# A closing projection that starts tile by tile in other PSUM banks, the last pair's transposes moved between the halves of its second unit, and finer waits in the first unit

## What is computed

```python
x = x + gnn(layernorm(x))     # 16 heads of 64; q, k, v projected twice; mask from 6144 edges
x = x + ffn(layernorm(x))     # 8 heads of 128, 8 experts per head, top 2 of them by a router
# in gnn, after the softmax:
out = attn @ v2               # 384 x 1024, two heads (a "pair") are 128 features
out = out @ wo.T + bo         # the closing projection
```

## Time and profile before

| | |
|---|---|
| median of 3 runs | 820.71 us (820.56 to 820.72) |
| the profiled execution | 820.65 us, of it the span from first to last instruction 818.9 us |
| TensorE busy | 808.5 us, 99% of the span |
| TensorE weight loads | 641.6 us, 78% |
| VectorE, ScalarE, GpSimd busy | 486.6, 370.3, 459.1 us |
| mean granted TensorE clock | 0.998 of full speed |
| moved by DMA | 153.50 MB, mean 187 GB/s |

### The profile page before, as it was taken

The page is one execution under the profiler, slowest core; times in us unless marked ns, Lnnn a source line. Parts: engine busy times, 40 slices in busy tenths (PEclk is TensorE's granted clock), DMA queues, the critical chain, the costliest instruction groups (busy, mean ns, idle before and its releaser), DMA issues.

```text
span 818.9 us, 13740 instructions
## 1 busy us (share of the span) xinstructions
PE 808.5 (99%) x4944; PEld 641.6 (78%) x4944; DVE 486.6 (59%) x1110; ACT 370.3 (45%) x599; POOL 459.1 (56%) x297
## 2 busy tenths in 40 slices
PE   8999999999998999999999999999999999999998
PEld 8999998988886779898588588588588488488476
DVE  7898860446564256998545545645645645645545
ACT  5433332566665343244634634535535535535531
POOL 4787776342423425557664664674664664664652
PEclk9999999999999999999999999999999999999999
DMA  8776565621222329634697696697697697697684
GB/s 295 201 218 186 187 167 159 204 90 66 78 79 71 104 79 341 204 107 144 134 265 264 142 284 237 145 264 257 145 270 250 136 269 257 141 256 261 150 219 171
DMA packets 73481, 153.50 MB, mean 187 GB/s; under 512 B 9520, under 2 KB 30640, under 8 KB 73424
## 3 DMA queue, kind: packets, MB, share of 16 engines
q1 hardware_dynamic: 59200, 120.93, 42.8%
q0 software_dynamic: 10944, 24.82, 16.8%
q10 hardware_dynamic: 3280, 6.98, 3.3%
HBM read 122.06 MB, written 37.97 MB: 195 GB/s over the span
## 4 chain that ended last, share of the span: by engine, by line
PE 96%; DVE 1%; DMA 1%; issue 1%; ACT 0%; POOL 0%; SPq 0%; DVEq 0%
PE bank L1651 26%; PE bank L1653 25%; PE bank L1652 25%; PE bank L1990 12%; PE bank L1706 2%; PE bank L1794 2%; PE bank L1769 2%; PE bank L1699 1%; DMA x<-in_x 1%; DVE stats L985 0%; PE bank L1741 0%; POOL rstd L538 0%; DVE x L1190 0%; PE bank L1747 0%; PE bank L1744 0%
## 5 line engine op out<-in xcount | busy, mean ns | idle before, releaser
L606 POOL TENSOR_TENSOR w_lo<-w_raw,w_hi 128x1024 fp32r<-128x1024 f32 x67 | 165.7, 2476 | 137.2 <-ACT w_hi L866 130.3
L1651 PE MATMUL bank<-w_hi,hT_hi 128*128 128x512 f32 x480 | 190.4, 397 | 4.1 <-DVE neg_mx L1127 3.2
L1653 PE MATMUL bank<-w_hi,hT_lo 128*128 128x512 f32 x480 | 188.2, 392 | 0.0
L1652 PE MATMUL bank<-w_lo,hT_hi 128*128 128x512 f32 x480 | 187.9, 391 | 0.0
L546 POOL TENSOR_TENSOR w_lo<-w_raw,w_hi 128x1024 fp32r<-128x1024 f32 x39 | 93.2, 2398 | 102.8 <-ACT w_hi L698 96.0
L866 ACT ACTIVATE w_hi<-w_raw 128x1024 fp32r<-128x1024 f32 x84 | 88.7, 1056 | 127.5 <-PE bank L1653 91.7
L1651 PEld LDWEIGHTS bank<-w_hi,hT_hi 128*128 128x128 f32 x480 | 91.0, 189 | 24.1 <-DVE neg_mx L1127 3.5
L1651 PE MATMUL bank<-hT_hi,w_hi 128*128 128x384 f32 x320 | 107.9, 337 | 0.0
L1652 PE MATMUL bank<-hT_lo,w_hi 128*128 128x384 f32 x320 | 107.0, 334 | 0.0
L1653 PE MATMUL bank<-hT_hi,w_lo 128*128 128x384 f32 x320 | 107.0, 334 | 0.0
L1653 PEld LDWEIGHTS bank<-w_hi,hT_lo 128*128 128x128 f32 x480 | 90.5, 188 | 19.3
(11 more groups left out here) (236 smaller groups left out, 1295.0 us busy)
## 6 DMA issues: line engine op xcount, KB each, us to landing
w_raw<-in_units SPq DMA_DIRECT2D x137, 512.0 KB
late<-in_units SPq DMA_DIRECT2D x56, 512.0 KB
w_raw<-in_units SPq DMA_DIRECT2D x16, 256.0 KB
scratch<-slots_scratch SPq DMA_DIRECT2D x7, 512.0 KB, 7.0
scratch<-in_src_row ACTq DMA_DIRECT2D x8, 384.0 KB
scratch<-in_dst_row ACTq DMA_DIRECT2D x8, 384.0 KB
sums_scratch<-zeros SPq DMA_DIRECT2D x1, 1536.0 KB, 8.0
sums_scratch<-x SPq DMA_DIRECT2D x1, 1536.0 KB, 10.6
```

The source lines that it names most:

```text
L606: pool.tensor_tensor(w_lo[:, s, :], w_raw[:, s, :], w_hi[:, s, :].bitcast(fp32), ALU.subtract).then_inc(lo_ready[s], 1)
L1651: pe.matmul(dst, a_hi, b_hi, start=first, stop=False)
L1652: pe.matmul(dst, a_hi, b_lo, start=False, stop=False)
L1653: return pe.matmul(dst, a_lo, b_hi, start=False, stop=last)
```

## The change

The first half of the closing projection is accumulated in banks 7, 6, 0 and the second in banks 3, 4, 5. Its unit 0 goes tile by tile (all six passes of a token tile together), starts after `oT_lo_done` of pair 6, and waits before the third tile alone for the first head's `max_ready`. Unit 1 is cut in two halves of 9 passes: head 0 of pair 7 is transposed between them, head 1 after them, both in banks 3 to 5, and pair 7 is attended in bank 1. At the start, the last `keep_warm` is 1 in place of 3, and the first and third pass of unit 0 wait for the last half tile only before block 4. SyncE issues the diagonal mask blocks ahead of the load of unit 5.

```diff
-WO_BANKS = ((3, 4, 5), (0, 1, 2))
+WO_BANKS = ((7, 6, 0), (3, 4, 5))
...
             for s in range(RING):
+                if s == RING - 1:
+                    sp.wait_ge(diagonal_ready, 1)
+                    for t in range(NT):
+                        sp.dma_start(mask_blocks[:, t, t, :], diagonal[:]).then_inc(no_edge_landed, 16)
                 sp.wait_ge(lo_ready[s], 1)
                 sp.dma_start(w_raw[:, s, :], units[RING + s]).then_inc(raw_landed[s], 16)
-            sp.wait_ge(diagonal_ready, 1)
-            for t in range(NT):
-                sp.dma_start(mask_blocks[:, t, t, :], diagonal[:]).then_inc(no_edge_landed, 16)
...
-            def oT_hi_of(pair):
+            def oT_hi_of(pair, at=6):
                 act.wait_ge(pair_out, pair + 1)
-                act.activation(oT_hi[:, pair, :], bank[6][:, 0:N], ACT.Identity,
+                act.activation(oT_hi[:, pair, :], bank[at][:, 0:N], ACT.Identity,
...
             hi_fixed(U_WO + 2)
-            pT_of(PAIRS - 1, 0, 0)
+            pT_of(PAIRS - 1, 0, 1)
             hi_fixed(U_WO + 3)
-            pT_of(PAIRS - 1, 1, 0)
+            pT_of(PAIRS - 1, 1, 1)
             hi_fixed(U_WO + 4)
-            oT_hi_of(PAIRS - 1)
+            oT_hi_of(PAIRS - 1, 1)
...
-            def oT_lo_of(pair, at, b):
+            def oT_lo_of(pair, at, b, src=6):
...
-            def row_unit(turns, u, banks, a_hi, a_lo, i, third=None, second_half=None):
-                s = unit_ready(turns, u)
-                for kk in range(2):
+            def row_unit(turns, u, banks, a_hi, a_lo, i, third=None, second_half=None, halves=(0, 1)):
+                s = unit_ready(turns, u) if 0 in halves else u % RING
+                for kk in halves:
...
-                last.then_inc(unit_used, 1)
+                if 1 in halves:
+                    last.then_inc(unit_used, 1)
...
-            keep_warm(3)
+            keep_warm(1)
             pe.wait_ge(hi_ready, 1)
-            pe.wait_ge(hT_hi_done, LN_STEPS)
             for k in range(KT):
+                if k % 4 == 0:
+                    pe.wait_ge(hT_hi_done, LN_STEPS - 1 + k // 4)
                 pe.matmul(bank[0][:, 0:N], w_hi[:, 0, k * P:(k + 1) * P], hT_hi[:, k, :], start=k == 0, stop=False)
             unit_ready(0, 0)
...
-            pe.wait_ge(hT_lo_done, LN_STEPS)
             for k in range(KT):
+                if k % 4 == 0:
+                    pe.wait_ge(hT_lo_done, LN_STEPS - 1 + k // 4)
...
-            def attend(pair):
+            def attend(pair, at=6):
...
-            pe.wait_ge(max_ready, PAIRS * 2)
-            project(0)
-            last_probs_of(PAIRS - 1, 0, 0)
-            first_probs_of(0, 0)
-            project(1)
+            def project_by_tiles():
+                s = unit_ready(0, U_WO)
+                for t in range(NT):
+                    if t == NT - 1:
+                        pe.wait_ge(max_ready, PAIRS * 2 - 1)
+                    for kk in range(2):
+                        tok = slice(t * P, (t + 1) * P)
+                        c = slice(kk * HALF, (kk + 1) * HALF)
+                        last = three(bank[WO_BANKS[0][t]][:, 0:HALF], oT_hi[:, kk, tok], oT_lo[:, kk, tok],
+                                     w_hi[:, s, c], w_lo[:, s, c], kk == 0, False)
+                last.then_inc(unit_used, 1)
...
+            pe.wait_ge(oT_lo_done, PAIRS - 1)
+            project_by_tiles()
+            project(1, halves=(0,))
+            last_probs_of(PAIRS - 1, 0, 1)
+            first_probs_of(0, 1)
+            project(1, halves=(1,))
             pe.wait_ge(pT_done, PAIRS * 6 - NT)
-            last_probs_of(PAIRS - 1, 1, 0)
-            first_probs_of(1, 0)
+            last_probs_of(PAIRS - 1, 1, 1)
+            first_probs_of(1, 1)
             project(2)
-            attend(PAIRS - 1)
+            attend(PAIRS - 1, 1)
             project(3, (oT_lo_done, PAIRS))
```

More of the change, by code:

```diff
@@ L1157, in k2_lo_of @@
                 split_lo(k2_lo[:], bank[7][:, 0:N], k2_hi[:], b, k2_lo_done)
-            def oT_lo_of(pair, at, b):
+            def oT_lo_of(pair, at, b, src=6):
                 dve.wait_ge(oT_hi_done, pair + 1)
-                split_lo(oT_lo[:, at, :], bank[6][:, 0:N], oT_hi[:, at, :], b, oT_lo_done)
+                split_lo(oT_lo[:, at, :], bank[src][:, 0:N], oT_hi[:, at, :], b, oT_lo_done)
             dve.wait_ge(rows_landed, 32 * (PAIRS + 1))
@@ L1185, in _ @@
             step.leave(PAIRS - 1)
-            oT_lo_of(PAIRS - 1, PAIRS - 1, bias[:, 5, PAIRS - 1:PAIRS])
+            oT_lo_of(PAIRS - 1, PAIRS - 1, bias[:, 5, PAIRS - 1:PAIRS], 1)
             def add_gnn(f, t):
@@ L1793, in attend @@
                         d = pair % 4 * P + GD * head
-                        last = pe.matmul(bank[6][GD * head:GD * head + GD, 0:N], values[pair // 4][:, m, d:d + GD],
+                        last = pe.matmul(bank[at][GD * head:GD * head + GD, 0:N], values[pair // 4][:, m, d:d + GD],
                                          pT[:, head, m, :], start=m == 0, stop=m == NT - 1)
@@ L1833, in _, with project @@
                 scores_of(j)
-            def project(n, second_half=None):
-                row_unit(0, U_WO + n, WO_BANKS[n // 4], oT_hi, oT_lo, n % 4,
-                         second_half=second_half)
-            pe.wait_ge(max_ready, PAIRS * 2)
-            project(0)
-            last_probs_of(PAIRS - 1, 0, 0)
-            first_probs_of(0, 0)
-            project(1)
+            def project_by_tiles():
[9 more added lines that the diff above has]
+                last.then_inc(unit_used, 1)
+            def project(n, second_half=None, halves=(0, 1)):
+                row_unit(0, U_WO + n, WO_BANKS[n // 4], oT_hi, oT_lo, n % 4, second_half=second_half, halves=halves)
+            pe.wait_ge(oT_lo_done, PAIRS - 1)
[4 more added lines that the diff above has]
+            project(1, halves=(1,))
             pe.wait_ge(pT_done, PAIRS * 6 - NT)
-            last_probs_of(PAIRS - 1, 1, 0)
-            first_probs_of(1, 0)
+            last_probs_of(PAIRS - 1, 1, 1)
+            first_probs_of(1, 1)
             project(2)
-            attend(PAIRS - 1)
+            attend(PAIRS - 1, 1)
             project(3, (oT_lo_done, PAIRS))
```

## The result

The changed kernel takes **815.65 us** (median of 6 runs, 815.14 to 816.91) against 820.69 us for the kernel before in the same comparison (6 runs, 819.01 to 821.0): a ratio of 0.9943, with a 95% interval from 0.993 to 0.9956. The prediction was 815.5 us, range 814.9 to 816.6.

What follows compares the result with a forecast made beforehand. TensorE was taken as the bound (96% of the chain), so only its work or waits count. Closing part 4.84 + first unit 0.1 + unit 6 0.2 = 5.1 us off 820.65 gives 815.5 us, range 814.9 to 816.6.

Steps and rivals of the forecast that it cites:

- The wait goes and nothing takes its place: Closing unit 0: starts 0.20 us after oT_lo of pair 6, ends at 259.05 in place of 263.89, saving 4.84 us.
- Two costs in one gap: Before closing unit 0: the wait for pair 7's second-head maxima costs 3.2 us, the slow clock behind it 1.6 us.
- The due times: Behind closing unit 0: each step meets its new due time; slack 1.6 us at head 0's rows, 0.9 at ScalarE's copies.
- The start gives most of its 0.5 us back at unit 2: First unit: gains 0.5 us, but unit 2 is held until 22.03 for GpSimd's low part; some 0.1 us is left.
- the rival in which the start keeps its whole 0.7 us: Start: unit 2's hold isn't real, so 0.5 and unit 6's 0.2 us come through, giving 815.1; chance 0.07.
- The diagonal: Start: mask diagonal issued earlier lands by 24.8, scatters start up to about 2 us earlier, unit 6's wait goes: 0.2 us.
- Behind the attention: After pair 7's attend: units 3 to 7, the adds and the layer norm move by the same 4.84 us.
- the second block been paced by its transfers or by GpSimd: Rival, second block: an earlier start would only lengthen a wait there, giving about 820.6; chance 0.03.
- The rival of the denser transposes: Closing part: denser transposes count as too little work, 3.4 us at 0.50 return and cost 1.6, giving 817.1; chance 0.04.
- a VectorE held up by the running TensorE: Rival, closing part: unit 0's PSUM writes delay head 0's normalised rows, TensorE stops before the transposes, kernel slower; chance 0.02.

Runs made afterwards that it cites:

- filling the gap alone: Kernel before, plus 13 dummy identity products (26 passes) into bank 7 while TensorE waits for the maxima: 818.99 us, ratio 0.9981.
- the key row moved: Changed kernel with VectorE's first key row moved behind the mask constants that release GpSimd: 815.44 us, ratio 0.993.
- both maxima ahead: Changed kernel, but unit 0 of the closing projection waits for both heads' maxima before its first pass: 820.49 us, ratio 1.0001.
- the start alone: Kernel before with only the changed start (finer waits, keep_warm of 1, diagonal mask blocks ahead of unit 5's load): 820.24 us, ratio 0.9997.

## Why the prediction was right

- **The wait goes and nothing takes its place.** Right. The term was 4.84 us; C measured 4.86. Unit 0 starts 0.20 us behind `oT_lo`, as the loop's row said, takes 4.22 us (forecast 4.23), and its wait for the first head's maxima costs nothing at the third tile (1.5 us ahead of the first, by the run with that wait moved).
- **Two costs in one gap, 3.2 and 1.6 us.** Right, and now separated: filling the gap alone gave 1.7 us by timing and 19.57 - 18.01 = 1.56 by C (272.38 - 254.37 = 18.01). But the 1.6 us are the price in the profiled execution, not a constant: in about a fifth of the runs the gap brings no slow stretch, and in another fifth a longer one (see the last section). The profile happened to be of the commonest kind, which is also that of the median. The forecast of the time after doesn't hang on this luck, as it takes off the slow stretch that the profile itself showed; the size of the gain does.
- **The due times.** Right. Slack of 1.6 us at the division and 0.9 at ScalarE's copies was forecast; neither showed a wait. In the profile the division ended 1.55 us before the transposes (258.19 + 1.08 against 260.82) and the copies 1.0 us before the second ones (261.76 + 1.09 = 262.85 against 263.85). The run without the cut took away the 2.1 us of nine passes and had its wait of 0.39.
- **The start gives most of its 0.5 us back at unit 2.** Right: unit 2's load at 22.01, forecast 22.03 (the prediction doesn't show how it comes to 22.03; its rows give 21.98 for the low part and 0.11 behind it). The part came to 0.23 us in place of 0.3. So the rival in which the start keeps its whole 0.7 us fell.
- **The diagonal.** Right in the mechanism, small in the share: 0.11 us, forecast 0.2. One term was mis-sized: the prediction took 4.0 us at most from issue to landing, and it was up to 5.7. Counted from the start of the last issue at 19.7 that is 25.4 at the latest, in place of 24.8, and GpSimd's own work ended at 25.47. So the landing came just in time. In the changed kernel taken again it took up to 6.0 us, and the first scatter began at 26.66, 1.24 us behind GpSimd's own work in place of 0.95; unit 6 had no wait there either. Some 0.9 us of that idling isn't the landing's: with the key row moved, GpSimd's own work ended at 26.39, later than any landing (25.5), and it still idled 0.91 us. The prediction has the 1 us between 25.52 and its forecast of 26.5 without saying where it comes from.
- **Behind the attention** everything moved by the same amount, but not to the last digit: from `attend` to the end there were 818.9 - 274.12 = 544.78 us before and 813.6 - 268.99 = 544.61 after. The changed kernel taken again had 813.7 - 268.94 = 544.76, and over all profiles this stretch is 544.61 to 544.87, with and without the change. So these 0.17 us are the spread of the stretch and no gain. Had the second block been paced by its transfers or by GpSimd, it would have grown by the 4.8 us; that rival fell.
- **The rival of the denser transposes** fell: the clock is 1.00 over both of them. So did the rival of a VectorE held up by the running TensorE: its distances from `oT_lo` to `neg_mx` and to the division are the same to 0.01 us.

## What to carry to other kernels

Look at an idle gap of the bound engine together with the granted clock behind it: here 3.2 us of waiting were 4.8 us of time, a gap of 1.5 us was only itself, and filling the longer one with dummy passes gave a third of the gain for two lines of code. One profile shows one execution: compare its mean granted clock with that of the other runs before you take a slow stretch's length as the price of a gap. When work is moved ahead, give each step behind it a new due time from the timelines, and split a unit where the next release falls inside it. A gain ahead of a step that another engine's own order releases is handed back there; ask which queue that engine stands in, and what else runs beside it, before moving it.

## What was not expected of the hardware

**The cost of a dropped clock is not constant.** After the same gap of 3.2 us the lower level lasted 3.4 us in the profile of the kernel before (the earlier trace rows show all but its edges) and about 6.8 us with both maxima ahead, the last 6.1 of them with TensorE at work, so that C was 19.57 and 20.84. The beginning differed too: with both maxima ahead the level was at 0.50 before unit 0 began, while in the kernel before unit 0 ran its first four passes at the higher one:

```profile
258.07:258.97 0.90, 0.90 (x4) 0.77 (x5) 0.69 (x3) 0.90 (x5) 0.00 (x0) 1.00 0.00 0
```

The single runs show that this is the spread of the kernels that keep the gap. There are 77 with their mean granted clock on record: 53 of the kernel before, 12 of the start alone and 12 with both maxima first. They fall into three groups:

| mean granted clock of the run | runs | time, median (lowest to highest) |
|---|---|---|
| 0.999 or 1.000 | 16 | 818.90 us (818.43 to 820.63; all but one at most 819.20) |
| 0.997 or 0.998 | 47 | 820.59 us (820.00 to 821.99) |
| 0.996 | 14 | 821.81 us (821.36 to 824.08) |

A stretch of 3.4 us at 0.50 lowers the mean over 819 us by 0.002, one of 6.8 us by 0.004, so the groups are those of no slow stretch, a short one and a long one; this assignment is worked out from the means, and only the last two groups have a profile. The filled gap (818.57 to 819.49, all 12 runs at 0.999 or 1.000) lies where the first group lies. Against the changed kernel's 815.65 us these are 3.2, 4.9 or 6.2 us more, the start's 0.2 to 0.3 us among them where it applies. The kernels without it spread over 0.5 to 1.8 us. What decides between the groups no run here shows. The Trainium skill (TensorE: Matmul & The Clock Gate, Part 1) says that the number of slow matmuls at a kernel's start differs from run to run; behind this gap in mid-kernel the traces agree (8 slow passes in the kernel before, 14 with both maxima first).

**VectorE and GpSimd block each other.** Beside GpSimd's subtraction a VectorE operation on 4 columns took 2.37 us in place of 0.15, and the subtraction itself, where it began while VectorE made the key row, 2.99 to 3.05 us in place of 2.4. The kernel before and the changed one have such meetings as well, at the cells of the scatters (6 columns, 0.17 us alone). The first piece's took 0.69 us before and 0.68 now. The second piece's took 0.17 before and meets the subtraction in the changed kernel, where it is hidden, as TensorE waits for nothing there:

```profile
34.63 2.86 DVE L1064 SCALAR_TENSOR_TENSOR cell<-scratch,key  x1
```

It ends at 37.49, as the subtraction does (37.45), though its row begins 0.41 us before the subtraction's; why, the profile doesn't show.

Before, with the scatters 2 us later, VectorE's `w_lo` at 37.71 met the subtraction and took 2.24 us. The Trainium skill (SBUF — State Buffer, Terms) says that the two engines share a port pair which one of them holds for a whole instruction while the other waits; by that rule, the trace agrees for operations with two inputs from SBUF, and the operations that read one from PSUM ran beside GpSimd at their usual length (in the changed kernel the comparison of 640 columns took 0.89 us at 20.31, beside the subtraction, and 0.88 at 31.20, where GpSimd only issues scatters).
